# Half-array products gathered into one block per pair, the w2 half group padded to 128 rows, and a contiguous maximum, in a graph-convolution kernel

## The chip, the cores and the metric

One Trainium2 chip, one core. The metric is the device time of one execution in microseconds; the kernel before has a median of 4837.28 us over 3 runs (4835.97 to 4840.45). DVE is VectorE, ACT is ScalarE, PE is TensorE, POOL is GpSimd, SP is SyncE.

## The reference, cut to what matters

Two layers on x of 16 images x 96 channels x 64 x 64, all float32.

```python
# layer 0: windows of 8x8 = 64 nodes, 9 nearest neighbours, edge MLP, max over the neighbours
y = affine(conv1x1(x, fc1_w, fc1_b), fc1_s, fc1_t)
nodes = windows(y, 8)                          # (1024, 64, 96)
idx = knn_idx(nodes, 9)                        # cosine distance, the node itself among them
x_j = nodes[idx]; x_i = nodes[:, :, None, :]
h = einsum('bnkc,oc->bnko', concat([x_i, x_j - x_i]), ew) + eb
h = max(gelu(h * es + et, exact), axis=2)      # (1024, 64, 192)
x = affine(conv1x1(windows_back(h), fc2_w, fc2_b), fc2_s, fc2_t) + x
# layer 1: inverted bottleneck
h = relu(bn1(einsum('oc,bchw->bohw', w1, x)))  # 576 channels
h = relu(bnd(depthwise3x3(h, wd)))
x = x + bn2(einsum('oc,bchw->bohw', w2, h))
```

## The kernel before, in words

The unit of work of layer 0 is a pair of windows: 32 pairs per image, 512 in all. For a pair, V = y x wV (the neighbour's part) and U = y x wU (the node's own part) stand together on 128 partitions in `VU`. `MV` holds the selector: for each window 8 x 64 one-hot columns that pick the neighbour's V row and the node's U row, and 64 more columns (slot KN) for the node itself. A product of `VU` with `MV` gives all pre-activations of 192 output channels for 8 neighbours x 64 nodes: `gather` parts 0 and 1 give the first 128 channels of window 0 and 1 (128 columns of the array), part 2 the last 64 channels of both windows, on 64 columns of the array each. `gather_self` (L544) does the same for the node itself: two products on 128 columns (L549), two on 64 (L552). The selector is made on the chip: `expand` (L503) multiplies features of the indices with a table into the PSUM tile `pone`, and ACT's `onehot` (L699, L706) applies a ReLU to it and writes `MV`, one activation per window, 512 elements on 64 partitions. Other products on 64 columns: `scores` (L475), `values` (L513, L524), and w1's last half group of 64 channels (L449). Those of w2's half group (L461) use 64 rows of the array.

ACT applies the GELU (`gelu`, L722, 512 elements for each of three parts; `gelu_self`, L728, 192 elements) and writes `g`, laid out [part][neighbour k][node n], 3 x 9 x 64 elements. DVE's `maxima` (L916) reduces over k, reading k innermost, so each read steps 64 elements (256 B). `g` has two buffers: the first GELU of pair P waits for `hid_ready`, the maxima of pair P - 2.

Layer 1 runs in strips of 16 rows beside layer 0: 8 pairs to a strip. ACT writes bn1 and ReLU into `hpad` (L653, L659, L672), starts the accumulator `acc` with tap 0 (L738) and ends it with bn and ReLU (L745); DVE adds taps 1 to 8 (`tap`, L930), 40 instructions a strip, 32 of 1024 elements and 8 of 512. 

All that shares the two PSUM banks `pmisc` is a job: fc1, ssq (sums of squares), inv (broadcast of inverse norms), fc2, w1, w2. `misc_jobs` gives each of the 32 pairs of an image 2 to 5 jobs in a fixed order, and `part_of` splits them into four parts between the steps of the pair. Job n on PE (`shared_job`, L383) waits for `misc_evac` n - 1: the evacuation, by ACT (`shared_evac`), of the job two before it. An fc1 job has two activations (L614, L617), each other job one; four `diag` activations (L753) of a chunk stand at 4 of 16 pairs. tap 0 and the last ReLU are spread over the strip's 8 pairs by `TAP0_AT`, `TAP0_LATE`, `RELU2_AT`.

The order of a pair P is written out by hand, each engine works in order, and semaphores tie them together:

- PE: scores(P+3), gather 0, jobs 0, expand(P+1), feature_transpose(P+2), gather 1, jobs 1, values(P+1), gather 2, jobs 2, gather_self, jobs 3.
- ACT: gelu 0, evacuation of jobs 0, one early tap 0, onehot(P+1), featT_copy(P+2), gelu 1, jobs 1, diagonals, vu_copy(P+1) (L713), gelu 2, feature_square(P+3) (L697), jobs 2, gelu_self, jobs 3, tap 0, ReLU.
- DVE: two taps, largest(P+3), xn, a tap, indices, a tap, feature_a, maxima(P-1), the remaining taps.

gather n waits for the GELU two before it (`pg` has two banks), gather 0 for onehot and vu_copy; feature_transpose(P+2) waits for the self GELU of pair P - 1.

Of the kernel before, what the change touches and what calls it, by code (L numbers as in the profile page):

```python
# [4 lines left out]
B, C, H, W = 16, 96, 64, 64  # L5
# [150 lines left out]
def build(nc, x, p97, p128, rows97, consts, consts128, consts16, out):  # L156
# [3 lines left out]
    with ctx:  # L160
# [33 lines left out]
        fc2T = w128[:, 0:3 * C].rearrange("p (k c) -> p k c", k=3)  # L194
        w2T = w128[:, 3 * C:8 * C].rearrange("p (g c) -> p g c", g=5)
        wd = w128[:, 8 * C:8 * C + 45].rearrange("p (g k) -> p g k", g=5)
        bnp = w128[:, 8 * C + 45:8 * C + 85].rearrange("p (n g) -> p n g", n=8)
        o_ = 8 * C + 85
        fc2s_row, g2_row, v2_row = (w128[:, o_ + k * C:o_ + (k + 1) * C] for k in range(3))
# [25 lines left out]
        VU = sb("VU", [128, 2, 2, O])  # L225
        MV = sb("MV", [128, 2, 2, KN + 1, NODES])
        g = sb("g", [128, 2, 3, KN + 1, NODES])
        gflat = g[:, 0].rearrange("p c k n -> p (c k n)")
        c16f = gflat[:, 0:C16]
        r97 = g[0:C + 1, 1].rearrange("p c k n -> p (c k n)")[:, 0:3 * O]  # L230
        hid = sb("hid", [128, 2, PPC, 3, NODES])
# [150 lines left out]
        def _(pe):  # L382
            def shared_job(b, p, k, job):  # L383
# [67 lines left out]
                else:  # L451
# [5 lines left out]
                    for gr in range(FULL):  # L457
                        nc.tensor.matmul(ps[0:C, 0:4 * W], w2T[:, gr, :], acc[:, par, gr, q * 4 * W:(q + 1) * 4 * W],  # L458
                                         start=(gr == 0), stop=False)
                    u = 64 * (q // 2)  # L460
                    nc.tensor.matmul(ps[0:C, 0:4 * W], w2T[u:u + 64, FULL, :],  # L461
                                     acc[u:u + 64, par, FULL, (q % 2) * 4 * W:(q % 2 + 1) * 4 * W],
                                     start=False, stop=False)
# [64 lines left out]
            def gather(P, p, part):  # L528
                n = 3 * P + part

                if due(count := n - 1):
                    pe.wait_ge(gelu_done, count)
                ps = pg[(3 * p + part) % 2]
                r = p % 2
                cols = [MV[:, r, w, 0:KN, :].rearrange("p k n -> p (k n)") for w in range(2)]
                if part < 2:
                    last = nc.tensor.matmul(ps[:, :], VU[:, r, part, 0:ONE128], cols[part], start=True, stop=True)  # L537
                else:
                    for w in range(2):
                        last = nc.tensor.matmul(ps[64 * w:64 * w + 64, :], VU[:, r, w, ONE128:O], cols[w],  # L540
                                                start=True, stop=True)
                last.then_inc(gather_ready, 1)

            def gather_self(P, p):  # L544
                r = p % 2

                pe.wait_ge(featT_evac, P + 3 if not isinstance(P, int) else min(P + 3, NPAIRS))
                for w in range(2):
                    nc.tensor.matmul(pself[:, 64 * w:64 * w + 64], VU[:, r, w, 0:ONE128], MV[:, r, w, KN, :],  # L549
                                     start=True, stop=True)  # L550
                for w in range(2):
                    last = nc.tensor.matmul(pself[64 * w:64 * w + 64, 128:192], VU[:, r, w, ONE128:O],  # L552
                                            MV[:, r, w, KN, :], start=True, stop=True)
                last.then_inc(self_ready, 1)
# [3 lines left out]
            def image(b, p0, p1):  # L558
                for p in range(p0, p1):
# [33 lines left out]

# [4 lines left out]
        def _(act):  # L598
# [100 lines left out]
            def onehot(P, p):  # L699
# [16 lines left out]
            def gelu(P, p, part):  # L716
                act.wait_ge(gather_ready, 3 * P + part + 1)
                if part == 0:

                    if due(count := P - 1):  # L720
                        act.wait_ge(hid_ready, count)
                nc.scalar.activation(g[:, p % 2, part, 0:KN, :],  # L722
                                     pg[(3 * p + part) % 2][:, :].rearrange("p (k n) -> p k n", k=KN),
                                     ACT.Gelu).then_inc(gelu_done, 1)

            def gelu_self(P, p):
                act.wait_ge(self_ready, P + 1)
                nc.scalar.activation(g[:, p % 2, :, KN, :],  # L728
                                     pself[:, 0:192].rearrange("p (c n) -> p c n", c=3),
# [33 lines left out]
            def image(b, p0, p1):  # L763
                for p in range(p0, p1):
# [47 lines left out]
        def _(dve):  # L812
# [32 lines left out]
            for r in range(2):  # L845
                for w in range(2):
                    v, u = 64 * w, 64 * (1 - w)
                    nc.vector.tensor_copy(MV[v:v + 64, r, w, KN, :], eye[v:v + 64, :])
                    step(nc.vector.tensor_copy(MV[u:u + 64, r, w, :, :],
                                               eye[u:u + 64, :].unsqueeze(1).to_broadcast([64, KN + 1, NODES])))  # L850

# [191 lines left out]
```

## Time and profile before

| what | value |
|---|---|
| median of 3 runs | 4837.28 us (4835.97 to 4840.45) |
| the profiled execution | 4838.94 us |
| its span | 4837.1 us |
| PE busy | 4619.9 us (96%) |
| DVE busy | 4693.2 us (97%) |
| ACT busy | 3791.8 us (78%) |
| POOL busy | 486.5 us (10%) |
| DMA | mean 17 GB/s |
| granted TensorE clock | 0.99 |

Busy is the time with at least one instruction of the engine in work. A product of float32 operands is two MATMUL rows in the trace (two passes). The ends of MATMULs are modelled, so distances between starts say more of PE than durations. Back-to-back instructions of ACT and DVE overlap by some tens of ns, so durations add up to more than busy time.

### The profile page before, as it was taken

The page shows a single profiled execution, that of the slowest core. Times are in us where ns is not written, and L with a number is a line of the kernel's source. Part 1 is how long each engine was busy: PE and PEld are TensorE (multiplying, and loading weights), DVE is VectorE, ACT ScalarE, POOL GpSimd, SP SyncE. Part 2 cuts the span into 40 slices and gives each one's busy share as a digit, 9 for nine tenths or more (in the row PEclk, how much of TensorE's full clock was granted, in tenths as well). Part 3 has the DMA queues.
Part 4 walks back from the last instruction along what each step waited for, and adds up shares of the span by engine and source line. Part 5 has one row for each costly group of instructions (what it writes and reads, how often), then busy time and mean ns, then how long its engine had stood idle before and what let it go on. Part 6 is the DMA issues. An engine that isn't in the chain of part 4 may idle for free.

```text
span 4837.1 us, 87468 instructions
## 1 busy us (share of the span) xinstructions
PE 4619.9 (96%) x28416; PEld 2567.8 (53%) x28416; DVE 4693.2 (97%) x5293; ACT 3791.8 (78%) x7749; POOL 486.5 (10%) x260
## 2 busy tenths in 40 slices
PE   5999999999999999999999999999999999999996
PEld 3555555555555555555555555555555555555543
DVE  3799999999999999999999999999999999999998
ACT  4878877887877878878878878878878788788773
POOL 0101101001011010111001010110100101110200
PEclk9999999999999999999999999999999999999997
DMA  1000000000000000010000000000000000100000
GB/s 44 14 16 19 11 26 11 19 19 18 17 14 24 11 21 17 11 28 11 18 21 12 23 13 18 19 18 19 13 24 11 21 17 11 28 11 11 14 6 12
DMA packets 33519, 83.58 MB, mean 17 GB/s; under 512 B 4674, under 2 KB 4930, under 8 KB 29956
## 3 DMA queue, kind: packets, MB, share of 16 engines
q1 hardware_dynamic: 33028, 77.38, 5.7%
q8 instruction: 265, 4.34, 0.4%
q14 instruction: 226, 1.85, 0.1%
HBM read 52.20 MB, written 25.17 MB: 16 GB/s over the span
## 4 chain that ended last, share of the span: by engine, by line
PE 55%; DVE 20%; issue 13%; ACT 10%; DVEq 0%; SPq 0%; DMA 0%; ACTq 0%; POOL 0%; POOLq 0%
DVE acc L930 13%; PE pg L537 11%; PE pmisc L458 8%; DVE hid L916 6%; PE pg L540 6%; PE pmisc L442 5%; PE pvu L524 4%; PE pself L549 3%; PE pmisc L466 2%; PE pmisc L461 2%; ACT diag L753 2%; PE pself L552 2%; ACT MV L706 2%; PE pmisc L403 2%; ACT g L722 2%
## 5 line engine op out<-in xcount | busy, mean ns | idle before, releaser
L930 DVE SCALAR_TENSOR_TENSOR acc<-hpad,w,acc 128x1024 f32<-128x1024 f32 (+1 forms) x2560 | 2917.3, 1174 | 25.8 <-ACT acc L738 25.8
L916 DVE TENSOR_REDUCE hid<-g 128x192 f32<-128x1728 f32 x512 | 1609.4, 3143 | 0.5 <-ACT g L728 0.5
L537 PE MATMUL pg<-MV,VU 128*128 128x512 f32 x2048 | 1149.5, 643 | 41.1 <-ACT VU L713 37.4
L722 ACT ACTIVATE g<-pg 128x512 f32<-128x512 f32 x1536 | 911.8, 594 | 239.4 <-DVE hid L916 150.9
L706 ACT ACTIVATE MV<-pone,cst 64x512 f32<-64x512 f32 x1024 | 694.6, 678 | 9.6 <-PE pone L510 0.4
L442 PE MATMUL pmisc<-x,w 96*128 96x384 f32 (+1 forms) x1536 | 649.3, 505 | 10.3 <-ACT hpad L653 5.7
L540 PE MATMUL pg<-MV,VU 128*64 128x512 f32 x2048 | 531.4, 595 | 36.2 <-ACT g L722 36.0
L653 ACT ACTIVATE hpad<-pmisc,sh,sc 128x384 f32<-128x384 f32 (+1 forms) x768 | 505.2, 658 | 47.2 <-PE pmisc L442 21.0
L458 PE MATMUL pmisc<-acc,w 128*96 128x256 f32 x2048 | 512.8, 394 | 25.2 <-ACT acc L745 22.8
L442 PEld LDWEIGHTS pmisc<-x,w 96*128 96x128 f32 x1536 | 268.9, 192 | 421.5 <-issue 297.2
L458 PEld LDWEIGHTS pmisc<-acc,w 128*96 128x96 f32 x2048 | 319.1, 165 | 290.4 <-issue 140.8
L524 PE MATMUL pvu<-wVU,y 97*64 97x192 f32 x4096 | 445.7, 338 | 0.0
L524 PEld LDWEIGHTS pvu<-wVU,y 97*64 97x64 f32 x4096 | 257.0, 136 | 323.0 <-issue 291.2
L745 ACT ACTIVATE acc<-acc,shd,scd 128x1024 f32<-128x1024 f32 (+1 forms) x320 | 361.2, 1150 | 15.7 <-DVE acc L930 15.4
L549 PEld LDWEIGHTS pself<-MV,VU 128*128 128x128 f32 x2048 | 308.3, 191 | 119.8 <-issue 35.0
L367 POOL COPY xs<-xn 96x512 f32<-96x512 f32 x128 | 165.7, 1295 | 1932.1 <-DVE xn L910 1932.1
L537 PEld LDWEIGHTS pg<-MV,VU 128*128 128x128 f32 x2048 | 309.1, 191 | 80.7 <-issue 51.3
L738 ACT ACTIVATE acc<-hpad,w 128x1024 f32<-128x1024 f32 (+1 forms) x320 | 339.0, 1060 | 0.0
L684 ACT ACTIVATE res<-pmisc,sc 96x256 f32<-96x256 f32 x256 | 119.6, 467 | 247.3 <-PE pmisc L466 245.7
L348 POOL TENSOR_SCALAR clamped<-ssq 128x16 f32<-128x16 f32 x32 | 93.2, 2911 | 2132.7 <-ACT ssq L624 2132.7
L549 PE MATMUL pself<-MV,VU 128*128 128x64 f32 x2048 | 286.5, 262 | 2.6 <-ACT featT L692 2.4
L697 ACT ACTIVATE feat<-feat 128x16 f16<-128x16 f16 x512 | 109.8, 214 | 220.9 <-DVE feat L897 218.5
(97 smaller groups left out, 5142.7 us busy)
## 6 DMA issues: line engine op xcount, KB each, us to landing
xin<-in_x_dram SPq DMA_DIRECT2D x32, 768.0 KB, 5.7
xres<-in_x_dram SPq DMA_DIRECT2D x128, 192.0 KB, 2.5
out_dram<-res SPq DMA_DIRECT2D x128, 192.0 KB, 2.1
g<-in_consts_dram SPq DMA_DIRECT2D x1, 640.0 KB
w<-in_p_dram SPq DMA_DIRECT2D x1, 570.5 KB
w<-in_p_dram SPq DMA_DIRECT2D x1, 259.2 KB
g<-in_rows_dram SPq DMA_DIRECT2D x1, 218.2 KB
cst<-in_consts_dram SPq DMA_DIRECT2D x1, 72.5 KB
```

What stands on the lines that cost most here:

```text
L442: last = nc.tensor.matmul(ps[:, o:o + (hi - lo) * W], w1T[:, gr * 128:(gr + 1) * 128], x1[:, lo:hi, :], start=True, stop=True)
L458: nc.tensor.matmul(ps[0:C, 0:4 * W], w2T[:, gr, :], acc[:, par, gr, q * 4 * W:(q + 1) * 4 * W], start=(gr == 0), stop=False)
L524: last = nc.tensor.matmul(pvu[h:h + 64, O * w:O * (w + 1)], nodes, wVU[:, k, :], start=True, stop=True)
L537: last = nc.tensor.matmul(ps[:, :], VU[:, r, part, 0:ONE128], cols[part], start=True, stop=True)
L540: last = nc.tensor.matmul(ps[64 * w:64 * w + 64, :], VU[:, r, w, ONE128:O], cols[w], start=True, stop=True)
L549: nc.tensor.matmul(pself[:, 64 * w:64 * w + 64], VU[:, r, w, 0:ONE128], MV[:, r, w, KN, :], start=True, stop=True)
L653: nc.scalar.activation(hpad[:, gr, r0:r1, 1:W + 1], ps[:, o:o + (r1 - r0) * W].rearrange("p (row col) -> p row col", col=W), ACT.Relu, bia ...
L706: last = nc.scalar.activation(MV[h:h + 64, p % 2, w, 0:KN, :], pone[h:h + 64, :, :], ACT.Relu, bias=nbias[h:h + 64, :], scale=1.0)
L722: nc.scalar.activation(g[:, p % 2, part, 0:KN, :], pg[(3 * p + part) % 2][:, :].rearrange("p (k n) -> p k n", k=KN), ACT.Gelu).then_inc(ge ...
L745: nc.scalar.activation(acc[:, par, gr, 0:n], acc[:, par, gr, 0:n], ACT.Relu, bias=shd[:, gr:gr + 1], scale=scd[:, gr:gr + 1]).then_inc(rel ...
L916: nc.vector.tensor_reduce(hid[:, c % 2, j, :, :], g[:, r].rearrange("p c k n -> p c n k"), op=ALU.max, axis=AX.X).then_inc(hid_ready, 1)
L930: nc.vector.scalar_tensor_tensor(out=dst, in0=src, scalar=wk, in1=dst, op0=ALU.mult, op1=ALU.add).then_inc(tap_done, 1)
```

## The change

Five edits. (1) `g` becomes [part][node][9] with k innermost, and the maxima read it contiguously; the GELUs write runs of 8 elements in rows of 9, the self GELU every ninth element. (2) The columns of `MV` go node by node with k innermost; the one-hot reads `pone` with a step of 64 elements and writes `MV` contiguously. The products read `MV` contiguously as before. (3) PE's order: jobs 1, 2 and 3 in a row, then self_full (the two full products), and then values, gather 2, self_half, which scores(P+4) of the next pair follow. self_full has a wait for the self GELU of the pair before. (4) ACT's order: jobs 1, diagonals, jobs 2 and 3, vu_copy, feature_square, gelu 2, gelu_self, tap 0, ReLU. (5) w2's half group is stored twice, once with zeros in the lower and once in the upper 64 rows, and multiplied on 128 rows; the parameter array grows by 96 columns (48 KB).

```diff
-        w2T = w128[:, 3 * C:8 * C].rearrange("p (g c) -> p g c", g=5)
+        w2T = w128[:, 3 * C:9 * C].rearrange("p (g c) -> p g c", g=6)
...
-        MV = sb("MV", [128, 2, 2, KN + 1, NODES])
-        g = sb("g", [128, 2, 3, KN + 1, NODES])
+        MV = sb("MV", [128, 2, 2, (KN + 1) * NODES])
+        g = sb("g", [128, 2, 3, NODES, KN + 1])
...
-                    u = 64 * (q // 2)
-                    nc.tensor.matmul(ps[0:C, 0:4 * W], w2T[u:u + 64, FULL, :],
-                                     acc[u:u + 64, par, FULL, (q % 2) * 4 * W:(q % 2 + 1) * 4 * W],
+                    nc.tensor.matmul(ps[0:C, 0:4 * W], w2T[:, FULL + q // 2, :],
+                                     acc[:, par, FULL, (q % 2) * 4 * W:(q % 2 + 1) * 4 * W],
                                      start=False, stop=False)
...
-            def gather_self(P, p):
+            def self_full(P, p):
                 r = p % 2
+                if due(count := P):
+                    pe.wait_ge(self_gelu, count)
                 pe.wait_ge(featT_evac, P + 3 if not isinstance(P, int) else min(P + 3, NPAIRS))
...
+            def self_half(P, p):
+                r = p % 2
                 for w in range(2):
...
                     for k in part_of(jobs, 1):
                         shared_job(b, p, k, jobs[k])
+                    for k in part_of(jobs, 2) + part_of(jobs, 3):
+                        shared_job(b, p, k, jobs[k])
+                    if valid(P, NPAIRS):
+                        self_full(P, p)
                     if valid(P + 1, NPAIRS):
                         values(P + 1, p + 1)
                     if valid(P, NPAIRS):
                         gather(P, p, 2)
-                    for k in part_of(jobs, 2):
-                        shared_job(b, p, k, jobs[k])
                     if valid(P, NPAIRS):
-                        gather_self(P, p)
-                    for k in part_of(jobs, 3):
-                        shared_job(b, p, k, jobs[k])
+                        self_half(P, p)
...
-                    last = nc.scalar.activation(MV[h:h + 64, p % 2, w, 0:KN, :], pone[h:h + 64, :, :], ACT.Relu,
+                    last = nc.scalar.activation(MV[h:h + 64, p % 2, w, 0:KN * NODES].rearrange("p (n k) -> p n k", k=KN),
+                                                pone[h:h + 64, :, :].rearrange("p k n -> p n k"), ACT.Relu,
                                                 bias=nbias[h:h + 64, :], scale=1.0)
...
-                nc.scalar.activation(g[:, p % 2, part, 0:KN, :],
-                                     pg[(3 * p + part) % 2][:, :].rearrange("p (k n) -> p k n", k=KN),
+                nc.scalar.activation(g[:, p % 2, part, :, 0:KN],
+                                     pg[(3 * p + part) % 2][:, :].rearrange("p (n k) -> p n k", k=KN),
                                      ACT.Gelu).then_inc(gelu_done, 1)
...
-                nc.scalar.activation(g[:, p % 2, :, KN, :],
+                nc.scalar.activation(g[:, p % 2, :, :, KN],
...
+                    for k in part_of(jobs, 2) + part_of(jobs, 3):
+                        shared_evac(b, p, k, jobs[k])
                     if valid(P + 1, NPAIRS):
                         vu_copy(P + 1, p + 1)
+                    if valid(P + 3, NPAIRS):
+                        feature_square(P + 3, p + 3)
                     if valid(P, NPAIRS):
                         gelu(P, p, 2)
-                    if valid(P + 3, NPAIRS):
-                        feature_square(P + 3, p + 3)
-                    for k in part_of(jobs, 2):
-                        shared_evac(b, p, k, jobs[k])
-                    if valid(P, NPAIRS):
                         gelu_self(P, p)
-                    for k in part_of(jobs, 3):
-                        shared_evac(b, p, k, jobs[k])
...
-                nc.vector.tensor_reduce(hid[:, c % 2, j, :, :], g[:, r].rearrange("p c k n -> p c n k"),
-                                        op=ALU.max, axis=AX.X).then_inc(hid_ready, 1)
+                nc.vector.tensor_reduce(hid[:, c % 2, j, :, :], g[:, r], op=ALU.max, axis=AX.X).then_inc(hid_ready, 1)
```

In the prologue DVE fills the constant half of `MV` in the new order, with one copy more per buffer and window.

## Rows read from the trace of the kernel before

**Rows 1.** Windows, 600:4200: length; busy us (count) PE, PEld, DVE, ACT, POOL; clock, DMA

```profile
600.00:4200.00 3600.00, 3512.33 (x21791) 1957.77 (x21788) 3581.65 (x4028) 2900.24 (x5933) 374.03 (x196) 1.00 0.06 18
```

**Rows 2.** Windows of line L916, the maxima, alone: busy us of DVE (count)

```profile
600.00:4200.00 3600.00, 1234.58 (x393) 1.00 0.06 18
...
140.00:4680.00 4540.00, 1562.20 (x498) 1.00 0.06 17
```

**Rows 3.** Waits, whole span: waiting line, waited for, us in total, times, longest

```profile
ACT g L722 <- DVE hid L916: 150.9, 141, 2.1
...
PE pg L537 <- ACT VU L713: 37.4, 70, 0.8
```

**Rows 4.** Groups of instructions by shape, DVE: busy us, mean ns, idle before

```profile
L930 DVE SCALAR_TENSOR_TENSOR acc<-hpad,w,acc 128x1024 f32<-128x1024 f32 x2048 | 2582.5, 1282 | 25.8 <-ACT acc L738 25.8
L916 DVE TENSOR_REDUCE hid<-g 128x192 f32<-128x1728 f32 x512 | 1609.4, 3143 | 0.5 <-ACT g L728 0.5
...
L930 DVE SCALAR_TENSOR_TENSOR acc<-hpad,w,acc 128x512 f32<-128x512 f32 x512 | 380.1, 742 | 0.0
```

**Rows 5.** Timeline, PE, 2431 to 2461: start us, duration us, line, columns, passes

```profile
2431.36 0.81 PE L442 MATMUL pmisc<-x,w 96*128 96x384 f32 x2
2432.10 0.87 PE L524 MATMUL pvu<-wVU,y 97*64 97x192 f32 x8
2432.80 1.03 PE L540 MATMUL pg<-MV,VU 128*64 128x512 f32 x4
2433.76 0.91 PE L442 MATMUL pmisc<-x,w 96*128 96x384 f32 x2
2434.51 0.56 PE L549 MATMUL pself<-MV,VU 128*128 128x64 f32 x4
...
2443.12 1.97 PE L458 MATMUL pmisc<-acc,w 128*96 128x256 f32 x8
2445.01 0.67 PE L461 MATMUL pmisc<-acc,w 64*96 64x256 f32 x2
2445.61 0.67 PE L466 MATMUL pmisc<-x,eye 96*96 96x256 f32 x2
2446.12 0.56 PE L549 MATMUL pself<-MV,VU 128*128 128x64 f32 x4
...
2447.99 0.81 PE L442 MATMUL pmisc<-x,w 96*128 96x384 f32 x2
2448.63 0.40 PE L510 MATMUL pone<-featT,c 128*128 128x64 f16 x8
...
2459.18 1.03 PE L420 MATMUL pmisc<-hid,w 128*96 128x256 f32 x4
2460.05 1.02 PE L422 MATMUL pmisc<-hid,w 128*96 128x512 f32 x2
```

**Rows 6.** Windows of two pairs, the 11th and 12th of their image, columns as rows 1

```profile
2173.16:2179.97 6.81, 6.81 (x47) 3.77 (x47) 6.38 (x11) 6.56 (x15) 1.42 (x1) 1.00 0.00 0
2179.97:2188.26 8.29, 7.80 (x59) 4.56 (x59) 8.29 (x9) 8.23 (x18) 0.00 (x0) 1.00 0.01 2
```

**Rows 7.** Timeline, ACT, 2180 to 2189: start us, duration us, line

```profile
2180.33 0.58 ACT L722 ACTIVATE g<-pg 128x512 f32<-128x512 f32 x1
2180.80 0.21 ACT L697 ACTIVATE feat<-feat 128x16 f16<-128x16 f16 x1
...
2181.46 0.33 ACT L728 ACTIVATE g<-pself 128x192 f32<-128x192 f32 x1
...
2187.52 1.26 ACT L753 ACTIVATE diag<-eye,inv 128x128 f32<-128x128 f32 x4
```

**Rows 8.** Groups of instructions by shape, ACT: busy us, mean ns, idle before

```profile
L706 ACT ACTIVATE MV<-pone,cst 64x512 f32<-64x512 f32 x1024 | 694.6, 678 | 9.6 <-PE pone L510 0.4
...
L728 ACT ACTIVATE g<-pself 128x192 f32<-128x192 f32 x512 | 166.8, 326 | 26.3 <-PE pself L552 24.5
...
L636 ACT ACTIVATE x<-pmisc,l0sc 96x512 f32<-96x512 f32 x128 | 86.9, 679 | 94.2 <-PE pmisc L426 94.2
```

More of the change, by code:

```diff
@@ L194, in build @@
         fc2T = w128[:, 0:3 * C].rearrange("p (k c) -> p k c", k=3)
-        w2T = w128[:, 3 * C:8 * C].rearrange("p (g c) -> p g c", g=5)
-        wd = w128[:, 8 * C:8 * C + 45].rearrange("p (g k) -> p g k", g=5)
-        bnp = w128[:, 8 * C + 45:8 * C + 85].rearrange("p (n g) -> p n g", n=8)
-        o_ = 8 * C + 85
+        w2T = w128[:, 3 * C:9 * C].rearrange("p (g c) -> p g c", g=6)
+        wd = w128[:, 9 * C:9 * C + 45].rearrange("p (g k) -> p g k", g=5)
+        bnp = w128[:, 9 * C + 45:9 * C + 85].rearrange("p (n g) -> p n g", n=8)
+        o_ = 9 * C + 85
         fc2s_row, g2_row, v2_row = (w128[:, o_ + k * C:o_ + (k + 1) * C] for k in range(3))
@@ L225, in build @@
         VU = sb("VU", [128, 2, 2, O])
-        MV = sb("MV", [128, 2, 2, KN + 1, NODES])
-        g = sb("g", [128, 2, 3, KN + 1, NODES])
-        gflat = g[:, 0].rearrange("p c k n -> p (c k n)")
+        MV = sb("MV", [128, 2, 2, (KN + 1) * NODES])
+        g = sb("g", [128, 2, 3, NODES, KN + 1])
+        gflat = g[:, 0].rearrange("p c n k -> p (c n k)")
         c16f = gflat[:, 0:C16]
-        r97 = g[0:C + 1, 1].rearrange("p c k n -> p (c k n)")[:, 0:3 * O]
+        r97 = g[0:C + 1, 1].rearrange("p c n k -> p (c n k)")[:, 0:3 * O]
         hid = sb("hid", [128, 2, PPC, 3, NODES])
@@ L534, in gather @@
                 r = p % 2
-                cols = [MV[:, r, w, 0:KN, :].rearrange("p k n -> p (k n)") for w in range(2)]
+                cols = [MV[:, r, w, 0:KN * NODES] for w in range(2)]
                 if part < 2:
@@ L542, in gather @@
                 last.then_inc(gather_ready, 1)
-            def gather_self(P, p):
+            def self_full(P, p):
                 r = p % 2
+                if due(count := P):
+                    pe.wait_ge(self_gelu, count)
                 pe.wait_ge(featT_evac, P + 3 if not isinstance(P, int) else min(P + 3, NPAIRS))
                 for w in range(2):
-                    nc.tensor.matmul(pself[:, 64 * w:64 * w + 64], VU[:, r, w, 0:ONE128], MV[:, r, w, KN, :],
+                    nc.tensor.matmul(pself[:, 64 * w:64 * w + 64], VU[:, r, w, 0:ONE128], MV[:, r, w, KN * NODES:],
                                      start=True, stop=True)
+            def self_half(P, p):
+                r = p % 2
                 for w in range(2):
                     last = nc.tensor.matmul(pself[64 * w:64 * w + 64, 128:192], VU[:, r, w, ONE128:O],
-                                            MV[:, r, w, KN, :], start=True, stop=True)
+                                            MV[:, r, w, KN * NODES:], start=True, stop=True)
                 last.then_inc(self_ready, 1)
@@ L847, in _ @@
                     v, u = 64 * w, 64 * (1 - w)
-                    nc.vector.tensor_copy(MV[v:v + 64, r, w, KN, :], eye[v:v + 64, :])
-                    step(nc.vector.tensor_copy(MV[u:u + 64, r, w, :, :],
-                                               eye[u:u + 64, :].unsqueeze(1).to_broadcast([64, KN + 1, NODES])))
+                    nc.vector.tensor_copy(MV[v:v + 64, r, w, KN * NODES:], eye[v:v + 64, :])
+                    nc.vector.tensor_copy(MV[u:u + 64, r, w, KN * NODES:], eye[u:u + 64, :])
+                    step(nc.vector.tensor_copy(MV[u:u + 64, r, w, 0:KN * NODES].rearrange("p (n k) -> p n k", k=KN),
+                                               eye[u:u + 64, :].unsqueeze(2).to_broadcast([64, NODES, KN])))
             es = r97[:, 0:O]
@@ L869, in _ @@
             step(nc.vector.tensor_tensor(fc2T, fc2T, fc2s_row.unsqueeze(1).to_broadcast([128, 3, C]), ALU.mult))
-            step(nc.vector.tensor_tensor(w2T, w2T, g2_row.unsqueeze(1).to_broadcast([128, 5, C]), ALU.mult))
+            step(nc.vector.tensor_tensor(w2T, w2T, g2_row.unsqueeze(1).to_broadcast([128, 6, C]), ALU.mult))
             step(nc.vector.tensor_tensor(sc2[:, 0:1], col97(V97 + 6), tmp2[:, 0:1], ALU.mult))
@@ L964 @@
 P97 = C + HID + 12
-P128 = 11 * C + 45 + 40
+P128 = 12 * C + 45 + 40
 CF = 81 + NODES
@@ L1001 @@
     zeros = np.zeros((O - ONE128, C), np.float32)
+    w2T = np.ascontiguousarray(l1("w2").T)
+    w2G = [w2T[k * 128:(k + 1) * 128] for k in range(FULL)]
+    w2G += [np.concatenate([w2T[FULL * 128:], zeros], 0), np.concatenate([zeros, w2T[FULL * 128:]], 0)]
     p128 = np.concatenate([
         fc2T[:ONE128], np.concatenate([fc2T[ONE128:], zeros], 0), np.concatenate([zeros, fc2T[ONE128:]], 0),
-        grouped(l1("w2").T).reshape(128, -1), grouped(l1("wd")).reshape(128, -1),
+        np.concatenate(w2G, 1), grouped(l1("wd")).reshape(128, -1),
     ] + [grouped(l1(n)).reshape(128, 5) for n in ("g1", "b1", "m1", "v1", "gd", "bd", "md", "vd")]
```

## The prediction

> **What bounds the kernel now.** I read the windows view first, over the steady part (600 to 4200 us). VectorE (DVE) is busy 3581.65 of 3600 us, 99.5%; TensorE (PE) 3512.33 us, ScalarE (ACT) 2900.24 us, at full clock [rows 1]. The same window holds 393 maxima, one per pair [rows 2], so a pair takes 3600/393 = 9.16 us, of which DVE works 9.11, PE 8.94, ACT 7.38. DVE sets the pace; it has no slack to give. But PE stands only 0.22 us behind it (its row also counts small waits, since the ends of products are modelled), and ACT waits for DVE, not the other way: 150.9 us before the first GELU, for the buffer that the maxima free [rows 3]. PE in its turn waits for ACT's copy of VU, 37.4 us [rows 3]. So a DVE gain shows only down to what PE needs, and the change must be priced on both, then on the ACT waits that come next.
>
> **DVE.** The maxima take 3143 ns for 1728 elements read 256 B apart. The taps take 1282 ns for 1024 and 742 for 512 elements in rows of 64, so 540/512 = 1.055 ns an element and 202 ns fixed [rows 4]. The maxima's own rate is (3143 - 202)/1728 = 1.70 ns. Read contiguously I take the taps' rate: 202 + 1728 x 1.055 = 2025 ns, 1.12 us less. Bounds: no gain (if the runs of 9 break the stream) and these 1.12 us. I take the upper end: the tap rows are the nearest, in one kernel column of three they too start at odd words, and the group keeps the rate. DVE then needs 9.11 - 1.12 = 7.99 us per pair and no longer sets the pace. The Trainium skill (Vector Engine (DVE) Microarchitecture Reference, 5.2 Measured stream behaviour on trn2) says that a port keeps its full rate on pairs of adjacent words and falls to about 1.73 ns when it hops at every element; the 1.70 above agrees. It gives 1.30 ns for pairs that start on an odd word; by that the maxima would take 2.45 us, and DVE, at 8.4 us, would still stand no higher than PE below.
>
> **PE, the switches.** A product that uses 64 columns of the array, or 64 rows, cannot follow a full one at once. Two full passes of 384 columns take 0.64 us until the next full product (2447.99 to 2448.63) and 0.74 until a 64-column one (2431.36 to 2432.10): 0.10 out, and I add 0.05, an estimate, for the first 64-column weights that are no longer hidden (half of the next number). Back: the same product after a 64-column block takes 0.75 instead of 0.64 (2433.76 to 2434.51), 0.11 for its weights, and the block ahead of it 0.96 where two passes of 512 columns, at the 0.87/4 that one of 256 takes, need 0.87: 0.09, taken as the 0.10 of the way out [rows 5]. In and out again: 0.36 us. From the job tables I counted the entries into a 64-column block over the whole program: 1151 before, 642 after. 509 x 0.36 = 183 us. For w2, eight passes, two on 64 rows and two more take 3.00 us (2443.12 to 2446.12), less about 0.08 (an estimate, as above) for the weights after the switch ahead of them; twelve full passes at the rate of the four that take 0.87 (2459.18 to 2460.05) take 2.61 [rows 5]. The padded half group costs no column more, so 0.31 to 0.39, taken as 0.34, x 256 jobs = 87 us. Together 270 us, or 0.53 per pair: PE needs 8.94 - 0.53 = 8.41 us. The bounds of this sum are 220 and 300 us.
>
> **The added wait** (self_full for self_gelu) costs nothing: feature_transpose, earlier in the same pair, already waits for that count. The block's own order is the dear part. Today the jobs of parts 2 and 3 come after values, gather 2 and the self products, so ACT has two to three us to clear a pmisc bank. After it, jobs 1, 2 and 3 follow one another, and in the 12 of 32 pairs that have four or more jobs the last one waits until ACT has evacuated the job two before it. Everything behind it on PE (self_full, values, gather 2) waits too, and ACT's gelu 2 waits for gather 2: a ring. Its length I read at the pair that starts at 2179.97. ACT runs from gelu 2 (2180.33) to the start of the diagonals (2187.52), through the tail of tap 0 and ReLU, gelu 0, the one-hot and gelu 1, without a gap [rows 7]: 7.19 us, less the 0.66 between 2180.80 and 2181.46 for steps that leave this stretch, 6.53. The PE leg behind it: last job 0.75, self_full 0.5, switch and values 0.1 + 0.70, gather 2 until its end 1.03, 0.1 of signalling (an estimate): 3.2 us [rows 5]. Sum 9.7, where that pair took 8.29 with ACT at 8.23 [rows 6], and PE would need about 7.7 (its 7.80 less small waits): 2.0 us of new wait. The same ring in pair 3 of the half image (a norm sum in place of the 0.4 us longer inverse) gives 9.3 against 7.7, in pair 2 (a shorter tail, but fc1's two activations) 9.3 against 8.3. In pair 10 ACT's own work, 7.6 by the same pieces with one diagonal set, exceeds PE's 6.6. ACT is already full there: 6.56 of 6.81 us and 8.23 of 8.29 [rows 6]. These 8 pairs of each image (2, 3, 10, 11, 18, 19, 26, 27) add 2 x (1.0 + 1.6 + 1.05 + 2.0) = 11.3 us, 0.35 per pair. In the others PE's jobs are long (w2, fc2) and the ring closes sooner.
>
> **ACT's changed accesses.** The one-hot reads PSUM 256 B apart and writes contiguously; the GELUs write runs of 8 in rows of 9, the self GELU single elements 36 B apart. No row shows ACT hopping at every element. Nearest is L636, which reads PSUM in runs of 8: 679 ns for 512, the same as the one-hot's 678 for 512 [rows 8]. Far end: the maxima's whole rate, 202 + 512 x 1.70 = 1072 ns, is 0.39 us more for each of the two one-hots, 0.79 per pair; likewise 202 + 192 x 1.70 = 528 ns for the self GELU's 326 [rows 8], 0.20; and if every second run of 8 pays the maxima's excess (1.70 - 1.055 = 0.65 ns) for starting at an odd word, 256 x 0.65 = 0.17 for each of three GELUs, 0.50. All three are 1.5 us per pair. A gain is excluded: the accesses replaced are contiguous already. I take zero, by the nearer row, and keep both ends. The prologue's extra copies and 48 KB of weights: at most 1 us, once.
>
> **The sum.** 8.41 + 0.35 = 8.76 us per pair against 9.16, 0.40 less, for the 498 pairs that lie between 140 and 4680 us [rows 2]: 199 us. Start and tail (the last strips' taps) stay. The profiled run took 4838.9 us with a span of 4837.1, 1.7 above the median of the three runs; 4838.9 - 199 + 1 = 4641, against the median 4639. I say 4640.
>
> **The rivals.**
> (a) PE alone: the ring is absorbed, since ACT has slack in most pairs. Then 8.41 + 0.05 and 0.70 x 498 = 349 us: 4490. For it: DVE reaches 99.5% today beside near-full partners. Against: the ring's parts already run without a gap [rows 7], and PE, once it is the bound, can't win back a wait.
> (b) The one-hot's strided read costs part or all of its 0.79 us per pair, on the ring: the 8 pairs lose it whole, 2 in 3 of the others little or nothing. 4700 to 4820.
> (c) Slower, one mechanism: ACT pays for every hop, in reads and writes, 1.5 us per pair. The 8 pairs lose 12 us more per image, and the others, where the ring is 0 to 1 us shorter than PE's need, some 11: (11.3 + 12 + 11)/32 = 1.07, so 8.41 + 1.07 = 9.48 us, 0.32 x 498 = 159 us slower, 5000. It decides from about 1.0 us per pair: 8 pairs x 1.0 and 4.6 in the others make (11.3 + 8 + 4.6)/32 = 0.75, the whole gain. The Trainium skill speaks for this one: Advanced Engine Details and Errata, PSUM Cachelines, wants every two consecutive elements next to each other and names a slowdown otherwise (for matmuls); no row of this trace shows the price for ACT.
> (d) The maxima don't get faster as the runs of 9 defeat the stream. DVE stays at 9.11 us: 4830, no change.
>
> **How the numbers follow.** Two kernels can be told apart by about 0.2%, 10 us. Forecast (4560 to 4700): 0.47. (a) 0.20. (b) 0.18, of which 0.01 ends within 0.2%. (c), at 1.0 us and beyond, 0.11. (d) 0.04, half of it within 0.2%. Faster: 0.47 + 0.20 + 0.17 + 0.01 = 0.85; same 0.01 + 0.02 = 0.03; slower 0.11 + 0.01 = 0.12. The range runs from 4470, which takes in nearly all of (a) with a larger switch price, to 4790, most of (b); outside stay (c), (d) and the ends.
>
> **What would show it.** Maxima near 2.0 us; DVE about 91% busy; no 64-row product and w2's twelve passes evenly spaced; gaps on PE before the last job of the four-job pairs, released by ACT's evacuation of pmisc, where today the waits are for VU; one-hot at 0.68 us. Wrong, if the one-hot reads over 0.8 us, if those gaps are absent (then (a)), or if the maxima stay above 2.5 us.

## The result, and the profile after

The changed kernel takes **4927.51 us** (median of 4, 4897.62 to 4939.86), where the kernel before takes 4836.96 on the same chip (4835.97 to 4840.45): ratio 1.0177, 95% interval 1.0128 to 1.0225. It is slower, though whether by 2% the interval leaves open, outside the range, and 287 us above the 4640 forecast. The profiled execution took 4919.95 us with a span of 4918.1 and a mean granted clock of 0.954 (0.990 before).

The windows view of the same steady stretch as in [rows 1], with the same columns, then that of the maxima alone as in [rows 2]:

```profile
600.00:4200.00 3600.00, 3385.29 (x21271) 2041.93 (x21271) 3057.46 (x3928) 2875.10 (x5797) 222.57 (x191) 0.95 0.06 17
...
600.00:4200.00 3600.00, 744.84 (x383) 0.95 0.06 17
```

383 pairs end there instead of 393: 9.40 us each. DVE fell from 3581.65 to 3057.46 us, as wanted, but PE is idle for 215 us where it was for 88, and works the rest at a clock that is no longer 1.00. Engines that all have slack and a kernel that is slower mean waits between them. The groups that answer to [rows 4, 8] (busy us, mean ns, idle before):

```profile
L932 DVE SCALAR_TENSOR_TENSOR acc<-hpad,w,acc 128x1024 f32<-128x1024 f32 x2048 | 2588.2, 1284 | 244.6 <-ACT acc L743 241.2 <-DVE acc L932 3.1
L919 DVE TENSOR_REDUCE hid<-g 128x192 f32<-128x1728 f32 x512 | 995.8, 1945 | 0.0
...
L727 ACT ACTIVATE g<-pg 128x512 f32<-128x512 f32 x1536 | 915.7, 596 | 221.4 <-PE pg L539 164.1 <-PE pg L536 55.0
L710 ACT ACTIVATE MV<-pone,cst 64x512 f32<-64x512 f32 x1024 | 695.1, 679 | 9.6 <-PE pone L509 0.3
L733 ACT ACTIVATE g<-pself 128x192 f32<-128x192 f32 x512 | 263.2, 514 | 0.0
```

The maxima take 1945 ns. The strided one-hot costs what it did (679 ns against 678); only the self GELU pays, 514 ns against 326. The waits, as in [rows 3] (us in total, times, longest):

```profile
ACT VU L718 <- PE pvu L523: 297.4, 438, 1.8
...
PEld pmisc L449 <- ACT hpad L657: 138.9, 66, 2.4
...
PE pmisc L449 <- ACT hpad L657: 100.1, 64, 1.9
...
PE pmisc L442 <- ACT hpad L657: 63.8, 35, 6.7
...
PE pmisc L458 <- ACT hpad L657: 23.8, 32, 3.5
```

The wait of the last job for ACT's evacuation of `pmisc` is there. At L449 it stands in pairs 3, 11, 19 and 27, four times per image and up to 1.9 us long; at L442 in pairs 2 and 18; and at L458, w2, in pairs 6 and 22, 0.6 us each time. ACT in its turn waits 297 us for the values behind it. That is the ring. The timeline of PE in pair 11 of an image (start, duration; in brackets the idle time before, and its releaser) shows what the ring does beyond waiting:

```profile
2227.30 1.12 PE L536 MATMUL pg<-MV,VU 128*128 128x512 f32 x2 [0.91 <-ACT VU L718]
...
2230.33 1.58 PE L442 MATMUL pmisc<-x,w 96*128 96x384 f32 x4
...
2233.79 1.32 PE L449 MATMUL pmisc<-x,w 96*64 96x320 f32 x4 [1.88 <-ACT hpad L657]
...
2235.04 1.12 PE L550 MATMUL pself<-MV,VU 128*128 128x64 f32 x4
2236.09 1.55 PE L523 MATMUL pvu<-wVU,y 97*64 97x192 f32 x8
2237.42 1.92 PE L539 MATMUL pg<-MV,VU 128*64 128x512 f32 x4
```

Gather 2 alone takes 1.92 us instead of 1.03 [rows 5]. Windows of the same pair (columns as rows 1; the clock is the third number from the end) say why:

```profile
2226.07:2233.60 7.53, 4.93 (x37) 2.71 (x33) 7.53 (x9) 7.47 (x15) 0.00 (x0) 1.00 0.00 0
2233.60:2235.00 1.40, 1.21 (x4) 0.28 (x4) 1.40 (x3) 1.40 (x7) 0.00 (x0) 0.59 0.00 0
2235.00:2239.34 4.34, 4.34 (x22) 2.62 (x22) 3.53 (x3) 1.66 (x5) 0.00 (x0) 0.50 0.00 0
```

PE had idled 0.91 us and then 1.88 us in this pair, 4.93 busy of 7.53; just after, the granted clock is 0.50, the lower of the two levels (1.2 GHz), though PE is busy all of the last 4.34 us. The Trainium skill (TensorE: Matmul & The Clock Gate, Part 1: The HAM clock gate) says that 1.2 GHz is the default state and activity of the array releases the throttle; this trace agrees: PE stays busy, and from 2241.00 us on the granted clock is back at 1.00. ACT's two GELUs 2 stand around it:

```profile
2227.06 0.59 ACT L727 ACTIVATE g<-pg 128x512 f32<-128x512 f32 x1
...
2233.64 1.27 ACT L758 ACTIVATE diag<-eye,inv 128x128 f32<-128x128 f32 x4
...
2239.39 0.60 ACT L727 ACTIVATE g<-pg 128x512 f32<-128x512 f32 x1 [1.11 <-PE pg L539]
```

From GELU 2 to the last job's start 6.73 us, from there to the next GELU 2 5.60: a ring of 12.33 us, against the 9.7 (6.53 and 3.2) of the prediction. The first leg is right, the second is not.

A second place was not in the prediction at all: the edge between two images, where the image loop of PE jumps back. PE's timeline after:

```profile
2120.20 0.28 PE L556 MATMUL pself<-MV,VU 128*64 128x64 f32 x4
2122.92 0.34 PE L486 MATMUL pscore<-xn,xs 97*64 97x64 f32 x4 [2.44 <-issue]
2123.25 1.12 PE L536 MATMUL pg<-MV,VU 128*128 128x512 f32 x2
...
2125.79 1.65 PE L442 MATMUL pmisc<-x,w 96*128 96x384 f32 x2 [1.42 <-issue]
2127.73 2.06 PE L536 MATMUL pg<-MV,VU 128*128 128x512 f32 x2
```

It waits 2.44 and 1.42 us for nothing that the profile shows ("issue"), and then its products take twice their time (gather 1.12 to 2.06 us for two passes; w1's two passes 1.65 instead of 0.81). The program has 13 such jumps: here the first wait is 1.90 to 2.54 us long, the second 0.32 to 1.97. Before, the wait ahead of the first scores was 0.81 to 1.32 us, with no second one; at one edge:

```profile
2373.81 0.33 PE L487 MATMUL pscore<-xn,xs 97*64 97x64 f32 x4 [0.93 <-issue]
```

The next table has the mean time of pairs of an image, from one pair's first scores product on PE to the next one's, over 14 images; all experiments below refer to it (us):

| pair | before | after | without ring, e9 | ring at full clock, e15 | predicted |
|---|---|---|---|---|---|
| 0 | 9.85 | 12.38 | 8.78 | 9.07 | |
| 2 | 8.93 | 11.44 | 8.93 | 10.39 | 9.3 |
| 3 | 7.61 | 10.48 | 7.61 | 9.37 | 9.3 |
| 6 | 10.22 | 10.15 | 9.89 | 10.15 | |
| 8 | 9.12 | 8.46 | 8.78 | 8.46 | |
| 10 | 6.80 | 6.92 | 6.80 | 6.92 | 7.6 |
| 11 | 8.30 | 12.23 | 8.36 | 10.68 | 9.7 |
| 16 | 9.01 | 8.36 | 8.68 | 8.36 | |
| all 32 | 293.2 | 300.0 | 281.2 | 285.5 | 280.3 |

Pairs 18, 19 and 27 of the second half image lie within 0.4 us of 2, 3 and 11 in every measured column. e9 is the old order with layout and padding, e15 the new order with the waits filled; both have PE's loop written out.

### The profile page after: what moved, and what is told of

Same layout as the page of the kernel before. It is cut to its first block, busy times and chain, and to the rows that moved or that the text cites. A ratio compares the mean times of both kernels' runs of the same rounds, so it can differ in the third digit from the quotient of the medians.

```text
span 4918.1 us, 87983 instructions
## 1 busy us (share of the span) xinstructions
PE 4537.9 (92%) x28416; PEld 2734.0 (56%) x28416; DVE 4107.1 (84%) x5297; ACT 3851.0 (78%) x7749; POOL 293.0 (6%) x260
## 4 chain that ended last, share of the span: by engine, by line
PE 80%; ACT 11%; issue 5%; DVE 3%; SPq 0%; DMA 0%; ACTq 0%; POOL 0%; DVEq 0%; POOLq 0%
PE pg L536 18%; PE pg L539 9%; PE pmisc L458 9%; PE pvu L523 8%; PE pmisc L442 6%; PE pself L550 4%; ACT MV L710 3%; DVE acc L932 2%; PE pmisc L411 2%; PE pone L509 2%; PE pmisc L396 2%; PE pmisc L426 2%; PE pmisc L420 2%; PE pmisc L422 2%; PE pmisc L465 2%
## 5 line engine op out<-in xcount | busy, mean ns | idle before, releaser
L536 PE MATMUL pg<-MV,VU 128*128 128x512 f32 x2048 | 1188.3, 663 | 30.3 <-ACT VU L718 28.4
L919 DVE TENSOR_REDUCE hid<-g 128x192 f32<-128x1728 f32 x512 | 995.8, 1945 | 0.0
L442 PE MATMUL pmisc<-x,w 96*128 96x384 f32 (+1 forms) x1536 | 619.5, 499 | 88.2 <-ACT hpad L657 63.8
L539 PE MATMUL pg<-MV,VU 128*64 128x512 f32 x2048 | 577.3, 643 | 0.0
L458 PE MATMUL pmisc<-acc,w 128*96 128x256 f32 x2048 | 499.9, 387 | 49.7 <-ACT acc L750 25.9
L442 PEld LDWEIGHTS pmisc<-x,w 96*128 96x128 f32 x1536 | 286.7, 195 | 459.5 <-issue 265.5
L883 DVE MAX8 top<-pscore 128x8 f32<-128x64 f32 x512 | 117.3, 229 | 496.7 <-PE pscore L488 492.6
L718 ACT ACTIVATE VU<-pvu 128x384 f32<-128x384 f32 x512 | 250.7, 490 | 297.9 <-PE pvu L523 297.4
L523 PE MATMUL pvu<-wVU,y 97*64 97x192 f32 x4096 | 480.7, 359 | 0.0
L458 PEld LDWEIGHTS pmisc<-acc,w 128*96 128x96 f32 x2048 | 331.2, 165 | 247.4 <-issue 106.3
L556 PEld LDWEIGHTS pself<-MV,VU 128*64 128x64 f32 x2048 | 155.3, 145 | 331.7 <-issue 331.7
L550 PE MATMUL pself<-MV,VU 128*128 128x64 f32 x2048 | 311.3, 276 | 29.1 <-ACT featT L696 29.1
```

Source lines behind the costliest of these rows:

```text
L442: last = nc.tensor.matmul(ps[:, o:o + (hi - lo) * W], w1T[:, gr * 128:(gr + 1) * 128], x1[:, lo:hi, :], start=True, stop=True)
L523: last = nc.tensor.matmul(pvu[h:h + 64, O * w:O * (w + 1)], nodes, wVU[:, k, :], start=True, stop=True)
L919: nc.vector.tensor_reduce(hid[:, c % 2, j, :, :], g[:, r], op=ALU.max, axis=AX.X).then_inc(hid_ready, 1)
```

## The experiments

Each was timed against the kernel before on the same chip. Ratios are to it, with 95% intervals. Several chips were used, on which the kernel before has medians of 4835.99 to 4839.65 us, so differences of a few us between experiments say nothing.

### The parts of the change alone

These four are cut out of the changed kernel. All of them keep the larger parameter array, and the added wait of `self_full` for `self_gelu`, which PE meets once per pair and which the kernel before lacks.

**e1_layout**: edits 1 and 2 alone (`g` node by node, one-hot strided), old order, w2's half group on 64 rows.

```diff
-        g = sb("g", [128, 2, 3, KN + 1, NODES])
+        g = sb("g", [128, 2, 3, NODES, KN + 1])
```

> Layout alone: the new g and MV with the contiguous maximum, the order of the kernel before and w2's half group on 64 rows. Ring theory (PE's last job waits for ACT's evacuation and then the clock halves; both come from the order): faster, PE is the bound at 8.9 us a pair, maxima 1.95 us, self GELU 0.51 us, hardly any half-clock stretch, 4700 to 4760 us. Layout theory (the strided self GELU and a DVE that runs ahead disturb the ring): 4830 or more, with half-clock stretches.

Measured: 4795.26 us, 0.9910 (0.9894 to 0.9927), clock 0.985: 35 us above the expected band. Its pair 0 takes 13.22 us, where before it was 9.85.

**e2_order**: edits 3 and 4 alone.

```diff
+                    for k in part_of(jobs, 2) + part_of(jobs, 3):
+                        shared_job(b, p, k, jobs[k])
+                    if valid(P, NPAIRS):
+                        self_full(P, p)
...
```

> Order alone: the new order of PE and ACT with the old layout and w2's half group on 64 rows. Ring theory: slower, DVE's 9.11 us a pair and the ring's waits add up: 5000 to 5100 us, half-clock stretches in pairs 2, 3, 11, 18, 19, 27 of an image. Layout theory: near 4840, since DVE sets the pace as before.

Measured: 5015.61 us, 1.0361 (1.0344 to 1.0378), clock 0.958, in the expected band. The halved clock stands in pairs 0, 2, 3, 11, 18, 19 and 27, as in the changed kernel. The order is what makes the change slow; the layout alone gains.

**e3_pad**: edit 5 alone. **e4_layout_pad**: edits 1, 2 and 5.

```diff
-                    u = 64 * (q // 2)
-                    nc.tensor.matmul(ps[0:C, 0:4 * W], w2T[u:u + 64, FULL, :],
+                    nc.tensor.matmul(ps[0:C, 0:4 * W], w2T[:, FULL + q // 2, :],
```

> w2's half group on 128 rows alone. DVE bounds the kernel before, so both theories expect 4820 to 4840 us, within 0.4%; w2's twelve passes should take 2.6 us in place of 3.0.

> Layout and padding with the order of the kernel before: the change without its order. Ring theory: the best of the four, PE needs 0.17 us a pair less than in the layout run: 4630 to 4700 us, no regular half-clock stretches. Layout theory: 4830 or more.

Measured: 4884.95 us, 1.0092 (1.0075 to 1.0108), a miss: padding alone is slower. And 4715.36 us, 0.9744 (0.9728 to 0.9760), for both, 15 us above its band. The miss of e3 is at the edge. PE's timeline of e3_pad there:

```profile
2096.76 0.34 PE L556 MATMUL pself<-MV,VU 128*64 128x64 f32 x4
2099.47 0.34 PE L486 MATMUL pscore<-xn,xs 97*64 97x64 f32 x4 [2.38 <-issue]
...
2102.32 1.65 PE L442 MATMUL pmisc<-x,w 96*128 96x384 f32 x2 [1.39 <-issue]
2104.26 2.05 PE L536 MATMUL pg<-MV,VU 128*128 128x512 f32 x2
```

The same two waits as in the changed kernel, and the same doubled products. Pair 0 goes from 9.85 to 12.91 us, pair 31 from 11.02 to 12.19, 4.2 us per image; other pairs give some back, and all 32 go from 293.2 to 296.4 us: 51 us in 16 images, where the kernel is 45 us slower. In e4 too pair 0 takes 12.33 us.

### Is it the wait, or the clock that it costs?

**e5_filler** and **e14_filler_one**: the changed kernel with two products (one in e14) that nobody reads, written into `pvu` ahead of the last job of the ring's pairs. They fill time in which PE waits anyway. If only the wait costs, nothing gets faster.

```diff
-                    for k in part_of(jobs, 2) + part_of(jobs, 3):
+                    for k in part_of(jobs, 2):
+                        shared_job(b, p, k, jobs[k])
+                    if p % 16 in (2, 3, 11) and valid(P, NPAIRS) and valid(P + 1, NPAIRS):
+                        for _ in range(2):
+                            nc.tensor.matmul(pvu[:, :], eye128[:, :], w128[:, 0:512], start=True, stop=True)
+                    for k in part_of(jobs, 3):
                         shared_job(b, p, k, jobs[k])
```

> The changed kernel with two more products (128x128 by 512 columns, 1.7 us at the full clock) that nobody reads, into the idle pvu bank, right before the last job of pairs 2, 3 and 11 of each half image, where PE stands idle for 1.9 us. Clock theory (the idle time itself costs little more than itself, but it halves the clock for what follows): the half-clock stretches in these pairs go, and although PE has 160 us more work, the time falls by 100 us or more, to 4750 to 4830. Wait theory (the ring alone sets the length of these pairs, the clock is a symptom): within 20 us of the changed kernel's 4927.

> One idle product (0.86 us) in place of the two of the filler run that took 4751. Clock theory with the clock falling only when PE idles long enough: between 4720 and 4760 if 1 us of remaining idle time no longer halves the clock, near 4850 if it still does in part of the pairs. Wait theory: 4900 or more.

Measured: 4751.15 us, 0.9815 (0.9799 to 0.9832), clock 0.991, and 4754.70 us, 0.9833 (0.9817 to 0.9850), clock 0.990. Adding work takes 176 us off. One product does as much as two, and pairs 2, 3 and 11 take the same in both (10.39, 9.37 and 10.68 against 10.39, 9.38 and 10.69): the products lie wholly inside the wait, and what came back is the clock. In e5 pair 0 also fell, to 9.03 us, though the loop was left as it was. The wait of the jump itself stayed; at one edge:

```profile
2056.14 0.34 PE L486 MATMUL pscore<-xn,xs 97*64 97x64 f32 x4 [2.25 <-issue]
```

Over the 13 edges it is 1.76 to 2.31 us, and pair 31, in whose time it falls, takes 9.78 us. The second wait is gone at all of them. Pair 0 takes 8.6 us with a clock of 1.00 at nine edges and 10.2 with a mean clock of 0.83 at four. So the halved clock does not follow from the jump's wait alone.

**e8_pe_unrolled**: the changed kernel with PE's image loop written out, so that PE has no jump back.

```diff
-            image_loop(pe, image, TAIL)
+            image(-1, 16, PAIRS)
+            for b in range(B):
+                image(b, 0, PAIRS)
+            image(B, 0, TAIL)
```

> The changed kernel with PE's loop over the images written out. Between pair 31 and pair 0 of the next image PE idles 2.4 and 1.4 us for nothing that the profile shows. If that is the jump back of PE's loop (edge theory): the wait and the half clock of pair 0 go, 4 us for each of 13 images, 50 us less: 4870. If it has another cause: no change, 4927.

Measured: 4870.15 us (4850.52 to 4888.63, 8 runs), 1.0066 (1.0043 to 1.0090): 57 us off, as expected. Pair 0 falls from 12.38 to 9.05 us, pair 31 from 10.05 to 7.82. The edge in its timeline:

```profile
2099.61 0.28 PE L556 MATMUL pself<-MV,VU 128*64 128x64 f32 x4
2099.72 0.29 PE L486 MATMUL pscore<-xn,xs 97*64 97x64 f32 x4
...
2100.93 0.81 PE L442 MATMUL pmisc<-x,w 96*128 96x384 f32 x2
```

No wait and no slow product. The Trainium skill (Runtime: NRT & Kernel Launch, Instruction fetch mechanics) says that a taken branch breaks the sequential prefetch of instructions and can stall; the edge agrees, since the wait is gone without the jump. Why the jump costs 0.93 us in one kernel, 2.25 in e5 and 2.4 and 1.4 in others stays open. The bodies of these loops differ for PE: that of the kernel before lacks the added wait in `self_full`, that of e5 has the filler's products besides. No run changed this alone.

**e15_filler_unrolled**: both, e8 with e5's two products.

> Two idle products and PE's loop written out, to be held against the changed kernel with the loop written out (4870), so that the image's edge is out of the comparison. Clock theory: the idle products alone still take off 100 us or more, 4730 to 4760 us. If most of the 176 us of the filler run came from the edge: over 4820.

Measured: 4718.69 us (4717.25 to 4721.19), 0.9760 (0.9743 to 0.9776), clock 0.993: 11 us below the expected band, and 151 us below e8, from unread work alone. Pair 11, in PE's timeline, with the filler as L591:

```profile
2143.70 1.74 PE L442 MATMUL pmisc<-x,w 96*128 96x384 f32 x4
2145.29 1.88 PE L591 MATMUL pvu<-w,eye 128*128 128x512 f32 x4
2147.33 0.76 PE L449 MATMUL pmisc<-x,w 96*64 96x320 f32 x4 [0.16 <-ACT hpad L665]
2148.02 0.66 PE L550 MATMUL pself<-MV,VU 128*128 128x64 f32 x4
2148.61 0.87 PE L523 MATMUL pvu<-wVU,y 97*64 97x192 f32 x8
2149.31 1.03 PE L539 MATMUL pg<-MV,VU 128*64 128x512 f32 x4
```

and in ACT's:

```profile
2140.60 0.59 ACT L735 ACTIVATE g<-pg 128x512 f32<-128x512 f32 x1
...
2147.17 1.27 ACT L766 ACTIVATE diag<-eye,inv 128x128 f32<-128x128 f32 x4
...
2150.38 0.60 ACT L735 ACTIVATE g<-pg 128x512 f32<-128x512 f32 x1 [0.26 <-PE pg L539]
```

GELU 2 to the last job is 6.73 us, as in the changed kernel; from there to the next GELU 2 3.05 instead of 5.60. The granted clock over this whole pair is 1.00, and the ring at full clock is 9.78 us, the prediction's 9.7.

### The ring itself

**e6_mid**: the half block, with scores(P+4) in it, put between jobs 1 and jobs 2, evacuations to match; meant to take the ring away and keep the switches saved.

```diff
-                    if valid(P + 3, NPAIRS):
-                        scores(b, P + 3, p + 3)
...
-                    for k in part_of(jobs, 2) + part_of(jobs, 3):
-                        shared_job(b, p, k, jobs[k])
                     if valid(P, NPAIRS):
                         self_full(P, p)
...
+                    if valid(P + 4, NPAIRS):
+                        scores(b, P + 4, p + 4)
+                    for k in part_of(jobs, 2) + part_of(jobs, 3):
+                        shared_job(b, p, k, jobs[k])
```

> The changed kernel with the block of half-array products, scores(P+4) included, between jobs 1 and jobs 2 instead of behind all jobs; ACT evacuates jobs 2 and 3 after the self GELU. The number of switches stays as low as in the changed kernel, but the last job no longer stands right behind the job whose evacuation it needs, with gather 2 behind it. Ring theory: 4600 to 4680 us, half-clock stretches only at the image's edge. Block theory (half-array products in one block leave the array half used for two us, and that halves the clock): half-clock stretches all over as in the changed kernel, over 4800.

Measured: 5392.10 us, 1.1132 (1.1113 to 1.1151), clock 0.940. The ring theory's number is missed by far. The block theory's (over 4800, low clock in many pairs) came true, but the waits explain it, and e16 below speaks against that theory: it keeps the block of half-array products and no pair of it has a lowered clock. The waits of e6:

```profile
PE pself L550 <- ACT featT L695: 594.9, 437, 3.2
...
DVE top L882 <- PE pscore L488: 802.4, 323, 7.0
```

self_full, now earlier, waits for ACT's copy of the transposed features in 437 pairs, and DVE 802 us for the scores, issued later. The move built a worse wait than it removed; as a test of the ring it says nothing.

**e13_j3_last**: the changed kernel with jobs 3 alone moved behind the half block. The last job then has values, gather 2 and the self products ahead of it; ACT evacuates it after the self GELU. **e16_j3_last_unrolled**: the same, loop written out.

```diff
-                    for k in part_of(jobs, 2) + part_of(jobs, 3):
+                    for k in part_of(jobs, 2):
                         shared_job(b, p, k, jobs[k])
...
                     if valid(P, NPAIRS):
                         self_half(P, p)
+                    for k in part_of(jobs, 3):
+                        shared_job(b, p, k, jobs[k])
```

> The changed kernel with jobs 3 alone taken back behind the half-array block; jobs 2 stay ahead of it. Ring theory (it is the last job's wait for the bank, with gather 2 behind it, that idles PE in pairs 2, 3 and 11): half-clock stretches there go, pairs 2 and 3 fall from 11.4 and 10.5 to about 9, the kernel to 4690 to 4760 us in spite of one switch pair more in 12 pairs of 32. If the block itself or jobs 2 are to blame: over 4850.

> Jobs 3 behind the half-array block, PE's loop written out. By the pair times of the run with jobs 3 last (278.7 us an image without the edge, against 281.2 of the old order with layout and padding, and 279.9 with jobs 3 ahead of the self products): 4590 to 4610 us, the fastest so far, 20 to 40 us under 4633.

Measured: 4699.25 us, 0.9717 (0.9698 to 0.9735), and 4616.23 us, 0.9549 (0.9533 to 0.9565), clock 0.993, 6 us above the expected band. Pairs 2, 3 and 11 fall to 9.61, 8.00 and 9.42 us without a filler. Moving one job in the 12 of 32 pairs that have a fourth part takes 228 us off the changed kernel (e13), and 102 us off e15, where the clock was already whole (e16). In e13 the ring's pairs are quick, but pair 0 still takes 12.21 us; with the loop written out it takes 9.05.

### The other order, and the best version

**e9_layout_pad_unrolled** and **e10_pad_unrolled**: e4 and e3 with PE's loop written out (edit as in e8).

> Layout and padding with the old order, PE's loop written out. Edge theory: pair 0 falls from 12.3 to about 8.7 us, 4715 becomes 4650 to 4670 us. Otherwise 4715.

> Padding alone, with PE's loop over the images written out. Padding alone was 1% slower than the kernel before, with pair 0 of an image at 12.9 us where it had 9.9, and half a clock there. Edge theory (PE, sooner done, idles longer at the jump of its loop, and the clock halves): 4820 to 4840 us, the slowdown gone. If the padding itself costs something: over 4860.

Measured: 4632.78 us, 0.9570 (0.9554 to 0.9586), 83 us below e4 and 17 below its band; and 4839.42 us (10 runs), 1.0007 (0.9997 to 1.0017), 46 us below e3. The slowdown of e3 lay in the edge: with the edge gone, padding alone is worth nothing, since DVE sets the pace. In its window DVE is busy all the time:

```profile
600.00:4200.00 3600.00, 3482.66 (x21808) 1990.17 (x21805) 3600.00 (x4029) 2899.24 (x5937) 508.73 (x196) 1.00 0.06 17
```

**e12_j3_before_self**: e9 with jobs 3 ahead of the self products (and their evacuation ahead of the self GELU), which then stand next to scores(P+4) of the next pair.

```diff
+                    for k in part_of(jobs, 3):
+                        shared_job(b, p, k, jobs[k])
                     if valid(P, NPAIRS):
                         self_full(P, p)
                         self_half(P, p)
-                    for k in part_of(jobs, 3):
-                        shared_job(b, p, k, jobs[k])
```

> Layout and padding, PE's loop written out, old order but for jobs 3, which go ahead of the self products, so that those stand directly before scores: one switch pair less in 12 of 32 pairs, and no product that a chain needs behind a bank wait but the self products. Ring theory: 30 to 70 us under the 4633 of the same kernel with jobs 3 last. If any job ahead of the self products delays ACT as in the changed kernel: over 4640.

Measured: 4613.29 us (4612.80 to 4616.06), 0.9539 (0.9523 to 0.9555), 20 us below e9, where 30 to 70 were expected. One pair of it still loses clock: pair 12, with a mean of 0.86, takes 10.32 us (10.05 in e9). It and e16 are the fastest, 4.6% and 4.5% below the kernel before; 3 us between kernels timed on different chips separate nothing.

## Why the prediction was wrong, step by step

**What bounds the kernel, and DVE: right.** The maxima take 1945 ns, 0.08 us below the 2025; runs of 9 don't break the stream. DVE no longer sets the pace. Rival (d) is out.

**The switches: right, a little smaller.** Where no ring interferes, the order alone (e15 against e9) takes 0.32 us off a pair: 8.78 to 8.46 in pair 8, 8.68 to 8.36 in pair 16. The prediction had 0.36. Padding takes 0.33 off pair 6 (10.22 before, 9.89 in e9), predicted 0.34. w2's twelve passes in the changed kernel:

```profile
2115.56 1.89 PE L458 MATMUL pmisc<-acc,w 128*96 128x256 f32 x8
2117.29 0.59 PE L460 MATMUL pmisc<-acc,w 128*96 128x256 f32 x2
2117.72 0.60 PE L465 MATMUL pmisc<-x,eye 96*96 96x256 f32 x2
2118.15 0.56 PE L550 MATMUL pself<-MV,VU 128*128 128x64 f32 x4
```

2.59 us (2115.56 to 2118.15), for 2.61 in the prediction and 3.00 before. By the prediction's own terms layout and padding without the order give 8.94 - 0.17 = 8.77 us per pair, 0.39 x 498 = 194 us less: about 4644. e9, which lacks the edge too, gives 4633; e4, with the loop as it was, 4715.

**ACT's accesses: right for the one-hot and the GELUs, wrong for the self GELU.** 679 and 596 ns, no price. The self GELU costs 0.19 us more, nearly the 0.20 of the far end. Rival (b) is out. So is (c): its sign came true, its mechanism did not, since ACT does not pay for hopping at every element when it reads PSUM, only in the one place where it writes single elements apart.

**Rival (a), the ring absorbed: out**, since even at full clock e15 stands at 4719, not 4490.

**The added order: the ring was seen, and its price was the failed step.** The releaser and the length of ACT's leg were right (6.73 us for 6.53), and at full clock so was pair 11's ring (9.78 us against 9.7). Of the places, pairs 2, 3, 11, 18, 19 and 27 were right; pairs 10 and 26 have only three jobs and show no such wait, and pairs 6 and 22, which the sum passed over, do. The step that failed is the "Sum 9.7" in the added wait: it prices a wait of PE at its own length and takes the 3.2 us of PE's leg from rows at clock 1.00. After a pair with 0.91 and 1.88 us of idle PE the granted clock is 0.50 and the leg takes 5.60. The first window [rows 1] showed a clock of 1.00 beside a PE that was busy 97.6% of it; whether it would hold with 2 us of new idle time was never asked. Of the 287 us missed:

- 151 us (e8 4870.2, e15 4718.7) are the halved clock in the ring's pairs and just behind them, shown by products that nobody reads.
- 57 us (4927.5, 4870.2) are the edge, with its own halved clock. "Start and tail stay" said nothing of the loop's jumps in between. The split between these two depends on the order: with the fillers put in first it is 176 (e5) and 32 (e5 to e15).
- 79 us (4718.7, 4640) are sizes in the sum. The eight pairs of the ring take 74.5 us per image in e15 (19.76 and 19.58 for 2, 3 and 18, 19; 17.60 and 17.51 for 10, 11 and 26, 27), where the prediction had 2 x (18.6 + 17.3) = 71.8: 2.7 us, 42 in 16 images. Most of it is pair 2, at 10.39 us for 9.3; pair 10 takes 6.92 for 7.6, pair 11 10.68 for 9.7. The switches' 0.04 us x 509 are 20. Pairs 6 and 22, where the sum saw no ring, take 10.15 with the last job ahead and 9.54 with it behind (e16): 1.2 us per image, 20. These make 82, an estimate from the pairs, not tested one by one; terms of the sum that came out better than forecast (e9's 4633 for 4644) are not in it.

This order thus does not pay even at full clock: with 0.32 x 509 = 163 us of switches saved, e15 is still 86 us slower than e9, so its waits cost some 249 (an estimate). The prediction had the two nearly equal (183 us of switches, 0.35 x 512 = 179 of ring). With the lower clock the net loss is 237 (e8 against e9).

**What would show it.** Gaps before the last job, w2 even, the one-hot at 0.68: as written. DVE at 91% came out at 85% (3057.46 of 3600), because pairs are longer.

## What to carry to other kernels

Price a new wait of TensorE twice: its own length, and the products behind it at the lower clock, if the engine is the bound and ran without gaps so far. Look at the granted clock in a window behind each of its waits, not only at its mean over the span (0.954 hides stretches at 0.50). When products are grouped to save a few tenths per switch, keep between two jobs that share a pair of buffers the work that gave their evacuation its time; here one job put back, in 12 of 32 pairs, was worth 228 us.

## What was not expected of the hardware

Unread work made the kernel faster by 151 to 176 us: one product per waiting pair, inside the wait, was enough to hold the clock at 1.00. Without it the clock fell behind idle stretches of 0.91 and 1.88 us. And e3, which differs from the kernel before on PE in the rows of some products and in one added wait per pair, has 2.38 and 1.39 us of waiting at a loop's jump where that had 0.93, and is 45 us slower; with the loop written out the same kernel stands at 1.0007 (0.9997 to 1.0017). Which of its differences does it was not tested.

For ACT, reading PSUM at a step of 256 B costs nothing (679 ns for 512 elements against 678), nor does writing runs of 8 in rows of 9 (596 ns per GELU), while writing 192 single elements 36 B apart takes 514 ns instead of 326.
